# Where fourteen projection tiles stand among the slots of an attention step

## The reference

```python
# layer 0: B=8, Sq=100, Sk=722, E=512, H=16 heads of 32
qn, kn, vn = layer_norm(x), layer_norm(ctx), layer_norm(ctx)
Q, K, V = heads(qn @ wq + bq), heads(kn @ wk + bk), heads(vn @ wv + bv)
out = softmax(Q @ K.T / sqrt(32)) @ V           # per batch and head
x = x + out @ wo + bo
x = x + gelu(layer_norm(x) @ w1 + b1) @ w2 + b2
# layer 1: heads of 64, context not normalised, no MLP
x = layer_norm(softmax(Q1 @ K1.T / 8 + c) @ V1 @ Wfc + x) * gamma + beta
```

## Time and profile before

| | us |
|---|---|
| median of 3 runs (lowest, highest) | 1609.01 (1606.13, 1609.79) |
| the profiled execution | 1609.01 |
| its span | 1607.2 |
| PE busy | 1385.7 (86%) |
| DVE busy | 857.0 (53%) |
| ACT busy | 685.6 (43%) |
| POOL busy | 514.8 (32%) |

### The profile page before, as it was taken

The page is one execution under the profiler, slowest core; times in us unless marked ns, Lnnn a source line. Parts: engine busy times, 40 slices in busy tenths (PEclk is TensorE's granted clock), DMA queues, the critical chain, the costliest instruction groups (busy, mean ns, idle before and its releaser), DMA issues. The chain is left out here.

```text
span 1607.2 us, 32652 instructions
## 1 busy us (share of the span) xinstructions
PE 1385.7 (86%) x12428; PEld 861.3 (54%) x12428; DVE 857.0 (53%) x1505; ACT 685.6 (43%) x1358; POOL 514.8 (32%) x580
## 2 busy tenths in 40 slices
PE   5457999899998656999929999999999999999968
PEld 3233556556655523544515666665666566666643
DVE  5735677667765466512524455454454455554554
ACT  2322666466565524310313444444444444444441
POOL 3100565556656762020001222222222222221134
PEclk9787999999999677999969999999999999999989
DMA  4275544453433043010484444444443334442221
GB/s 139 60 151 116 127 87 100 106 114 90 109 68 83 2 132 119 27 66 27 157 172 103 99 104 99 104 86 98 91 91 82 80 86 99 103 87 64 57 86 63
DMA packets 217261, 149.97 MB, mean 93 GB/s; under 512 B 148608, under 2 KB 190080, under 8 KB 217104
## 3 DMA queue, kind: packets, MB, share of 16 engines
q1 hardware_dynamic: 217104, 147.81, 39.0%
HBM read 59.29 MB, written 10.65 MB: 44 GB/s over the span
## 5 line engine op out<-in xcount | busy, mean ns | idle before, releaser
L649 POOL TENSOR_TENSOR attn_probs<-attn_p,attn_probs 128x400 f16<-128x400 f32 (+1 forms) x288 | 282.6, 984 | 653.0 <-ACT attn_probs L964 648.9
L1057 DVE TENSOR_REDUCE attn_nmax<-attn_p_max 100x1 f32<-100x722 f32 x256 | 232.2, 907 | 155.4 <-PE attn_p_max L821 152.0
L799 PE MATMUL attn_p_proj<-attn_ctxT,kv_w_k 128*128 128x361 f16 x1536 | 257.2, 323 | 35.6 <-DMA attn_ctxT<-attn_out_o_upper 29.7
L804 PE MATMUL attn_p_proj<-kv_w_v,attn_ctxT 128*128 128x512 f16 (+1 forms) x1152 | 264.3, 379 | 0.0
L954 ACT ACTIVATE attn_p<-attn_p_sc,attn_score_bias 128x400 f32<-128x400 f32 x192 | 113.5, 591 | 287.2 <-PE attn_p_sc L850 287.2
L799 PEld LDWEIGHTS attn_p_proj<-attn_ctxT,kv_w_k 128*128 128x128 f16 x1536 | 146.2, 99 | 126.5 <-issue 33.0
L964 ACT CAST attn_probs<-attn_p 128x400 f16<-128x400 f32 (+1 forms) x384 | 197.7, 517 | 0.0
L804 PEld LDWEIGHTS attn_p_proj<-kv_w_v,attn_ctxT 128*128 128x128 f16 (+1 forms) x1152 | 110.3, 101 | 111.1
L954 ACT ACTIVATE attn_p<-attn_p_sc 128x400 f32<-128x400 f32 x192 | 96.3, 502 | 147.7 <-PE attn_p_sc L846 137.4
L804 PE MATMUL attn_p_proj<-l_w_v,attn_ctxT 128*128 128x512 f16 (+1 forms) x576 | 136.3, 388 | 18.2 <-DVE attn_vbuf L1087 18.2
L1087 DVE SCALAR_TENSOR_TENSOR attn_vbuf<-attn_p_proj,attn_vbuf 128x512 f16<-128x512 f32 x144 | 99.4, 690 | 95.9 <-ACT attn_vbuf L982 94.9
(11 more groups left out here) (175 smaller groups left out, 2355.2 us busy)
## 6 DMA issues: line engine op xcount, KB each, us to landing
attn_kstack_a<-attn_knat SPq DMA_DIRECT2D x128, 180.5 KB, 3.6
attn_kstack<-attn_knat SPq DMA_DIRECT2D x192, 90.2 KB, 2.2
attn_kstack_b<-attn_knat SPq DMA_DIRECT2D x64, 180.5 KB, 3.9
attn_c<-in_ctx_dram SPq DMA_DIRECT2D x40, 256.0 KB, 3.5
kernel_w_qo<-in_ctx_dram SPq DMA_DIRECT2D x35, 256.0 KB, 3.0
rows_wo_w<-in_L_xattn_w_dram SPq DMA_DIRECT2D x8, 512.0 KB, 4.0
cols_w_w<-in_L_xattn_w_dram SPq DMA_DIRECT2D x4, 1024.0 KB, 5.7
q_stack<-mlp_hT SPq DMA_DIRECT2D x16, 200.0 KB, 2.8
```

The source lines that it names most:

```text
L649: eng.tensor_tensor(probs[:r, g % 2, 1, t, :HG * SQ], p32[:r, t % 3, :], probs[:r, g % 2, 0, t, :HG * SQ], ALU.subtract).then_inc(p_lo_mad ...
L799: last = pe.matmul(bank[:, :HALF], w_k[:, wa, k, c0 + m * P:c0 + (m + 1) * P], ctxT[:, cpar, ca, k, n * HALF:(n + 1) * HALF], **flags)
L804: last = pe.matmul(bank[:r, :], ctxT[:, cpar, ca, k, P * t:P * t + r], w_v[:, wa, k, c0:c0 + E], **flags)
L1057: dve.tensor_reduce(nmax[:SQ, hh:hh + 1], p_max[:SQ, :, :HALF], AX.XY, ALU.max, negate=True).then_inc(max_made, 1)
```

## The change

One list of numbers is edited: the slots of the fourteen projection tiles of layer 0.

```diff
-        at = [0, 1, 2, 3, 6, 7, 8, 9, 12, 13, 14, 18, 19, 20] if layer == 0 else [0, 0, 1, 1, 2, 2, 3, 3, 4, 6, 7, 8, 10, 11]
+        at = [0, 1, 3, 4, 6, 7, 9, 10, 12, 13, 15, 16, 18, 21] if layer == 0 else [0, 0, 1, 1, 2, 2, 3, 3, 4, 6, 7, 8, 10, 11]
```

## The result

| | before | changed |
|---|---|---|
| median of 4 runs (lowest, highest) | 1608.35 (1606.13, 1609.79) | 1623.98 (1619.97, 1628.02) |
| the profiled execution, its span | 1609.01, 1607.2 | 1620.46, 1618.7 |
| ratio of medians, 95% | | 1.0098 (1.007 to 1.0127) |

The changed kernel is slower by 15.6 us, by its interval 11 to 20. The forecast was 1617, 8 us slower: the direction was right, the size was half of what was measured, and the measured median lies 0.02 inside the upper end of the range. The same kernel measured again in a later session, with six runs (1622.30 to 1636.83), gave 1626.02 against 1607.82, ratio 1.0124 (1.0098 to 1.0151).

The account below looks back on a forecast made before the run. PE was taken as the engine to keep fed, so only its idle time could move. Steady steps +4.75, step 7 +4.2, step 8 +1.0 and step 0 -1.0 gave +8.95 us, 1618.0, lowered to 1617; range 1608 to 1624.

Parts of the forecast that it names:

- the first stretch: Slots 0 to 7 of a steady step, bound by DVE: 15.45 us to become 15.35, +0.8 and -0.9.
- What goes: PE waits in slots 16 and 22 (0.84 each), 18 (1.22) and 20 (0.2) disappear: 3.1 us a step.
- The steady step: One of steps 2 to 6, three stretches summed: +0.95 us each, bounds -0.3 and +1.8; 4.75 for five.
- second stretch: Slots 7 to 13 of a steady step: 13.93 us to become 14.9, +0.95, as K tile 6 moves behind the output transposes.
- third: Slot 13 to the next slot 0: 3.2 us of new waits against 3.1 that go, +0.1.
- Step 7: The step that prepares no further context: about 6.9 us of waiting instead of about 2.6, +4.2.
- Step 8: The step without projections, starting with its first reduction late: +1.0 us, between 0 and 1.0.
- Steps 0 and 1: Step 0: V bank released earlier, two more maxima ahead, about -1.0 us; step 1 comes out even.
- the third rival: The clock falls in slots 19 to 21, 1.4 us a time, six steps: +8.5, 1625; chance 0.13.
- The good trade: Evacuations stay out of the reductions' way, steady steps gain 1.7 us each: 1601 at best, or 1605; chance 0.12.
- the even case: Same gaps, but step 7 loses only +2.1 us and output transposes come 0.5 earlier: 1606 to 1612; chance 0.17.
- The mutual exclusion of VectorE and GpSimd: Slot 19's low part may meet POOL's subtraction, making slot 21's wait 0.75 us longer in five steps: 1621.

Follow-up runs that it names:

- old_in_7: The changed kernel, but with the list of before in step 7 only; 1619.65 us, ratio 1.006 to the kernel before.
- four_moved: The changed kernel with K tile 3 in slot 5, K6 in 8, K7 in 9 and V13 in 20; 1597.89 us, ratio 0.9933 to the kernel before.
- k6_in_8: The changed kernel with K tile 6 back in slot 8, all else as changed; 1624.22 us, ratio 1.009 to the kernel before.
- v13_in_20: The changed kernel with V tile 13 back in slot 20; 1614.46 us, ratio 1.0029 to the kernel before.
- v_part: The kernel before with only the V tiles as changed, K tiles in their old slots; 1618.27 us, ratio 1.005 to the kernel before.

## Why the prediction was right, and where it was wrong

The direction and the named gaps were right; the size was not, because two steps of the sum failed. One is the premise that the change can move PE's idle time "and nothing else": it moved the clock too, and the sum had nothing for that (4.7 us measured). The other is the first stretch, where DVE was to win back 0.9 a step: -0.1 was forecast and +0.33 came, 2.2 us over five steps. The rest is mostly steps 0, 1 and 8 (2.1). That the median still lies within the range, by 0.02, is luck; that of the later session, 1626.02, does not.

**PE waits make the steps: right, but not the whole.** PE's busy time hardly changed (1385.7 to 1389.2, with more of it under the lower clock) and every step's growth is found in PE's gaps and the lower clock.

**What goes: right.** 0.84 twice, the 1.22 of slot 18 and the V bank's wait are gone in each steady step. The V bank's wait had been 0.2 in the step that I read, but 0.2 to 0.9 over steps 2 to 6.

**What comes, gap by gap: right.** By the starts, forecast and measured: slot 3, 0.6 and 0.61 to 0.70 (1.13 in step 4); slot 7, 0.4 and 0.33 to 0.41; slot 9, 0.9 and 0.88; the output transposes, 1.55 and 1.52; slot 15, 0.61 and 0.61; slot 20, 0.98 and 0.98; slot 21, 1.6 to 2.0 and 1.34 to 2.27; slot 1, 0.5 and 0.43 to 0.76 (1.67 in step 4, right behind the loop's turn and partly under the lower clock). All of steps 2 to 7.

**The steady step: right in two stretches, wrong in the first.** Lengths from maximum to maximum, as the forecast cuts them, in steps 2 to 6 against those of before, on average and without the two falls: second stretch (slots 7 to 13) +0.96 (forecast +0.95), third (13 to 0) +0.13 (+0.1), first (0 to 7) +0.33 (-0.1). That is the step that failed here. I had set the late reduction of slot 0 (+0.8) against 0.9 that DVE would win back in a chain that binds from slot 0 to 7. What came are PE's own waits in slots 1, 3 and 4, 1.65 in step 2, against 1.4 less in slots 0, 6 and 7. The +0.13 hides two misses that cancel: slot 21 waited 1.83 on average where I took 1.6, and more of the V bank's wait went. Altogether, from start to start, a step grew by 1.44 without the clock, not 0.95: 7.2 for five steps, not 4.75.

**Step 7: right.** +4.16 without the clock's 1.50 (forecast +4.2); old_in_7 bears it out.

**Step 8: too small**, +2.0 for +1.0. Its second maximum, PE at 536.96, does wait 0.99 longer than the 1.13 of before:

```profile
534.50 0.34 PE L846 MATMUL attn_p_sc<-attn_qstack,attn_kstack 104*128 104x100 f16 x4
536.96 0.51 PE L821 MATMUL attn_p_max<-attn_kstack,attn_qstack 96*100 96x361 f16 x2 [2.12 <-DVE attn_nmax L1057]
```

That is the forecast's +1.0. The other 1.0 I can only argue: the lower clock now begins 3.6 us into the step, and 9.0 before.

**Steps 0 and 1: sign wrong**, +1.5 and -1.4 for -1.0 and 0. The last V tile of step 0, which answers to the earlier trace rows, and the maximum ahead of it:

```profile
143.16 0.84 PE L821 MATMUL attn_p_max<-attn_kstack,attn_qstack 96*100 96x361 f16 x2 [3.12 <-DVE attn_nmax L1057]
143.80 5.31 PE L804 MATMUL attn_p_proj<-l_w_v,attn_ctxT 128*82 128x512 f16 x12
```

The wait of 2.99 behind the last context tile did not go: the maximum of slot 21 inherits it as 3.12, and the tile starts 2.9 later than before, under the lower clock. In four_moved, where the tile stands ahead of that maximum, it started at 139.44 and took 2.75. Step 1 got most of it back: its first K tile took 3.67 at 148.40 before, at the lower clock, and runs at 149.89 and full clock now. Together the two steps cost +0.1 where the forecast had -1.0.

**The clock: the term that was left out of the sum.** It stood only as the third rival (0.13, 1625), six falls at 1.4. There were three, which cost 1.68, 1.53 and 1.50 by the starts, 4.7 in all; step 2 has much the same gaps and none. Only the first stands behind slots 19 to 21, where the rival put all six; the other two stand behind slots 8 and 9. So the rival named the mechanism, and its 1625, the number nearest to the result, is in part luck. The 4.7 are half of the 9.2 by which my 8.95 fell short of the stage's 18.2; the steady steps' share is 2.5 (2.2 of it in the first stretch), that of step 8 1.0, of steps 0 and 1 1.1. I had the evidence: the earlier trace rows shows the clock falling after 1.85 us of work in 3.40, and I wrote that slots 19 to 21 would be thinner, and then gave it one chance in eight.

The Trainium skill, "TensorE: Matmul & The Clock Gate", section "Why this matters for your kernels", wants no long idle gaps between bursts of matmuls, and gaps of two microseconds would pass by it. The trace disagrees: three falls came with a longest idle time of 1.4 to 2.1. The same page's section "A second HAM failure mode: psum-queue depth-cycling" tells of a kernel whose many short idle times between groups of matmuls made the clock swing; that is what these rows show, for waits on one PSUM buffer.

**Slips in the recorded sums.** In the second stretch 0.49 + 1.85 + 0.86 is 3.20 and not 3.24, and the upper bound of a steady step comes to about +1.65 from its own two terms and not +1.8. Neither moves the forecast.

**The rivals.** The good trade (1605) and the even case (to 1612) are refuted, by the gaps. The mutual exclusion of VectorE and GpSimd (1621; the Trainium skill, "SBUF — State Buffer", section "Who interferes with whom") didn't touch the place I named: from 195 to 500 us all low parts of context tiles ran at full speed, as this view of line 1049 says (minimum, median, maximum in ns):

```profile
L1049 DVE SCALAR_TENSOR_TENSOR attn_cparts<-attn_c,attn_rstd,attn_cparts x30: 736/743/752, 223.0 to 471.9; 128x512 f16<-128x512 f32 x25, 82x512 f16<-82x512 f32 x5
```

In k6_in_8 it did, in slot 9: the low part of 1.49 at 279.83, shown above, starts together with a subtraction on POOL, and the 0.75 that it lasts longer are part of the wait for `misc`. From 195 to 500 us ten of the thirty low parts took 1.44 to 1.50 in the kernel before, five in k6_in_8 and none in the changed kernel: where the tiles stand decides whether the two meet. POOL's timeline of k6_in_8:

```profile
279.83 0.94 POOL L649 TENSOR_TENSOR attn_probs<-attn_p,attn_probs 128x400 f16<-128x400 f32 x1 [0.81 <-ACT attn_probs L964]
```

**What stays open.** The time of a run varies with no edit: 1619.97 to 1628.02 for the changed kernel and 1622.30 to 1636.83 in the later session, and its two profiled executions (1620.46 and 1622.30) lie at the low end. Whether the slower ones have more falls no trace shows. Nor is it settled why k6_in_8, v13_in_20, v_part and old_in_7 have more falls than the changed kernel, or why one thin stretch is followed by a fall and its twin of another step is not.

## What to carry to other kernels

When work is moved between the slots of an engine that must be fed, list for every slot what it waits for and what now stands in front of it, each semaphore and each shared buffer included: here one bank used for two purposes (1.88 us a step) decided between a kernel 0.1% under the one before and one 0.7% under it. A single PSUM buffer with a reader on another engine needs cover between each two uses (1.47 us here); take it from a place only if the place has another. And where an edit makes stretches thinner than one behind which the trace already shows the clock falling, put falls into the sum (1.5 to 1.7 us each here), not into a rival; how many will come these runs could not tell.

## What the runs showed of the hardware that was not expected

- The granted clock fell after stretches in which PE was busy 1.47 to 1.74 of 3.40 us (the four that are shown), with no idle time over 2.11; each fall made PE's work behind it 1.5 to 1.7 us longer. 80 useless matmuls a step kept it at 1.00 in these places and made the kernel faster.
- The falls stood in the same places in two profiles of one program from two sessions (within 0.1 us once the start is lined up), but moved with a small edit: 3, 4, 6, 6 and 9 falls in the changed kernel, v13_in_20, v_part, old_in_7 and k6_in_8.
- At the turn of the hardware loop PE stood idle for 3.1 to 4.4 us, put down to issue and to no other engine; the clock fell there in ten of eleven profiles, and held in the one with the shortest idle time (3.06).
- Attention of layer 1, which no kernel edited, took from 719.9 to 725.1 us, and 720.1 and 723.1 for one and the same program. Differences of a few microseconds between two profiled executions must be sought in the edited stage, not in the span.
